# TensorE's attention loop as fourteen bodies written out, in a gated cross-attention and feed-forward kernel

## The reference, cut to what matters

```python
x = x + tanh(g_xattn) * mha(layernorm(x), ctx, ctx)      # x, ctx: 32 x 256 x 512, 16 heads of 32
x = x + tanh(g_ffn) * ffn(layernorm(x))                  # ffn: 512 -> 1408 (silu(gate) * up) -> 512
# mha: q, k, v projections with bias, softmax(q k^T / sqrt(32)) v, output projection with bias
# ffn: weights and activations are rounded to 8-bit grids; the scale of the activations
# is the maximum over the whole tensor, so each of its two quantisations needs a pass of its own
```

## Time and profile before

| | us |
|---|---|
| three runs | 1904.65, 1897.21, 1901.03 |
| their median | 1901.03 |
| the profiled execution's own time | 1898.31 |
| its span, first to last instruction | 1896.1 |
| PE's granted clock, mean of the span | 0.951 of full speed |
| T of body 1, start of body 2 | 191.4 |
| T of body 15, start of body 16 | 1269.4 |

### The profile page before, as it was taken

The page is one execution under the profiler, slowest core; times in us unless marked ns, Lnnn a source line. Parts: engine busy times, 40 slices in busy tenths (PEclk is TensorE's granted clock), DMA queues, the critical chain, the costliest instruction groups (busy, mean ns, idle before and its releaser), DMA issues.

```text
span 1896.1 us, 34665 instructions
## 1 busy us (share of the span) xinstructions
PE 1645.5 (87%) x11820; PEld 782.3 (41%) x11868; DVE 1402.2 (74%) x1853; ACT 813.1 (43%) x1068; POOL 516.7 (27%) x782
## 2 busy tenths in 40 slices
PE   3769989989999899998999899986599999989787
PEld 2224434434344344443444434433344444434333
DVE  6627687787877868768778687786778778878565
ACT  2223524325144152342432514324677777756242
POOL 6212414324133242331422423112000000006644
PEclk7979999999999999999999999998799999999899
DMA  6445454454444444445445444315235453115997
GB/s 190 127 119 116 121 147 110 121 138 120 126 109 121 135 119 125 115 119 148 110 121 127 128 126 93 94 55 204 89 142 192 166 214 140 45 45 212 340 420 301
DMA packets 271525, 274.48 MB, mean 145 GB/s; under 512 B 156720, under 2 KB 205872, under 8 KB 268848
## 3 DMA queue, kind: packets, MB, share of 16 engines
q1 hardware_dynamic: 271408, 272.73, 47.4%
HBM read 126.10 MB, written 62.39 MB: 99 GB/s over the span
## 4 chain that ended last, share of the span: by engine, by line
issue 63%; POOL 13%; DVE 9%; PE 6%; DMA 4%; SPq 2%; POOLq 1%; ACT 0%; DVEq 0%; ACTq 0%
DMA x<-out_dram 4%; DVE rs L873 3%; POOL ol L545 3%; POOL xres L552 3%; POOL yh L600 3%; PE bank L1264 2%; DVE mx L881 2%; SPq L358 1%; PE bank L1165 1%; POOL nw L527 1%; PE bank L1167 1%; PE bank L1166 1%; POOLq L259 1%; POOL nw L525 1%; POOL nw L529 1%
## 5 line engine op out<-in xcount | busy, mean ns | idle before, releaser
L873 DVE RECIPROCAL rs<-bank 128x256 f32<-128x256 f32 x128 | 224.5, 1754 | 125.7 <-POOL ol L545 105.5
L639 ACT ACTIVATE pr<-spair 128x1024 f32<-128x1024 f32 x256 | 258.9, 1019 | 112.0 <-PE spair L1246 112.0
L881 DVE TENSOR_REDUCE mx<-spair 128x4 f32<-128x1024 f32 x256 | 300.0, 1213 | 0.0
L632 ACT ACTIVATE parts<-bank,bqk 128x512 f16<-128x512 f32 x128 | 87.9, 687 | 293.9 <-PE bank L1167 293.9
L1264 PE MATMUL bank<-pr,v 128*32 128x256 f32 x2048 | 140.5, 392 | 54.8 <-DVE o L875 54.8
L1361 PE MATMUL spair<-xqT,wgT 128*128 128x512 bf16 x684 | 179.5, 382 | 2.8 <-ACT xqT L747 1.8
L1361 PE MATMUL spair<-xqT,wuT 128*128 128x512 bf16 x691 | 179.9, 381 | 0.7
L860 DVE SCALAR_TENSOR_TENSOR parts<-bank,bqk,parts 128x512 f16<-128x512 f32 x128 | 95.1, 748 | 114.6 <-ACT parts L632 114.6
L1246 PE MATMUL spair<-stacks 128*128 128x256 f16 x1024 | 154.1, 277 | 7.8 <-DMA stacks<-mT 7.3
L1165 PE MATMUL bank<-xT,wqT 128*128 128x512 f16 x256 | 103.2, 403 | 58.8 <-issue 24.7
L730 ACT ACTIVATE sil<-spair,gsc 128x512 f32<-128x512 f32 x176 | 118.1, 680 | 75.2 <-PE spair L1361 75.2
(11 more groups left out here) (160 smaller groups left out, 3198.6 us busy)
## 6 DMA issues: line engine op xcount, KB each, us to landing
stacks<-parts SPq DMA_DIRECT2D x768, 64.0 KB, 2.0
x<-out_dram SPq DMA_DIRECT2D x32, 1024.0 KB, 11.2
h_spill<-hb SPq DMA_DIRECT2D x10, 2816.0 KB, 9.2
hb<-h_spill SPq DMA_DIRECT2D x10, 2816.0 KB, 15.2
xbuf<-in_x_dram SPq DMA_DIRECT2D x16, 1024.0 KB, 5.4
cbuf<-in_ctx_dram SPq DMA_DIRECT2D x16, 1024.0 KB, 6.0
xres<-in_x_dram SPq DMA_DIRECT2D x16, 1024.0 KB, 5.3
out_dram<-xres SPq DMA_DIRECT2D x16, 1024.0 KB, 4.3
```

What stands on the lines that cost most here:

```text
L639: act.activation(pr[:, u % 4, :, :, :].rearrange("p a b q -> p (a b q)"), spair[u % 2][:, :, :].rearrange("p a q -> p (a q)"), ACT.Exp, sc ...
L873: dve.reciprocal(rs[:, g % 2, :], obank[:, S:2 * S]).then_inc(recip_done, 1)
L881: dve.tensor_reduce(mx[:, h:h + 2, b, :], spair[u % 2][:, :, :].rearrange("p a (q k) -> p a q k", q=KH), AX_X, ALU.max).then_inc(max_done, 1)
```

## The change

PE's loop over i from 1 to 7, with two bodies in each iteration, becomes fourteen bodies in a row. The loop is a Python `for` now, which writes its instructions out when the program is built. PE's branch and its loop register are gone, the values in the waits are constants, and so the `waits_passed` increments behind the waits marked `alone` aren't issued by PE in these bodies. The matmuls, their order and what each waits for are the same. The programs of the other engines are the same.

```diff
             body(1, 0, 1, None)
-            with pe.Fori(1, NG // 2) as i:
-                body(2 * i, 2 * i - 1, 0, 2 * i - 2)
-                body(2 * i + 1, 2 * i, 1, 2 * i - 1)
+            for i in range(2, NG):
+                body(i, i - 1, i % 2, i - 2)
             body(None, NG - 1, None, None)
```

## The result

| | before | after |
|---|---|---|
| median of 20 runs, us | 1902.67 | 1891.76 |
| lowest to highest | 1892.04 to 1911.60 | 1888.75 to 1897.21 |
| ratio after to before, 95% interval | | 0.9948 (0.9933 to 0.9962) |
| span of the profiled execution | 1896.1 | 1890.6 |

The kernel got faster, by 0.52% in the ratio and by 10.9 us in the medians, where 17.0 were forecast and 8.0 to 26.0 lay inside the range. The twenty runs of after also lie in less than half the width of the twenty before.

What follows compares the result with a forecast made beforehand. PE, the fullest engine, was taken as the bound. Bodies 4 to 14 go from 853.0 to 829.4 plus 6.6 for the clock, 836.0: 17.0 us saved, profiled 1881.3, plus 2.7 for the median, 1884.0; range 1875 to 1893.

Steps and rivals of the forecast that it cites:

- The six turns: Seams ahead of bodies 4, 6 to 14: each loop turn costs 3.3 us net at the second `pv`; all six go.
- Rival B: At the seams: the stall is not the turn's; only 1.4 us go, time 1900 us; chance 0.06.
- D: Rival in bodies 2 to 15: fetching straight code starves PE; 1944 us at 1 us per late packet; chance 0.03.
- The clock's term: Last third of bodies 4 to 14: lower granted clock costs 1.2 us in 5.5 of eleven bodies, 6.6 us.
- The ends: Limits of the lower-clock cost in bodies 4 to 14: none of them pays, or all eleven do.
- only two lengths: Odd bodies take either 75.4 us at clock 1.00 or 76.6 us at 0.98, nothing else.
- Constants instead of registers: Waits in the fourteen bodies: constants change nothing; at the end 0.15 us a body either way, 2 us.
- Rival C: Bodies 4 to 15 all pay 1.2 us of clock, constants cost 2 us: 7.2 us gained, 1894 us; chance 0.09.
- A: The forecast case: six turns go, the clock's cost falls on some bodies; 1877 to 1891 us; chance 0.81.

Runs made afterwards that it cites:

- the tiny loops at the seams: Written-out kernel with a two-pass loop of one semaphore increment at each of the six seams where the loop used to turn: 1892.15 us, ratio to before 0.9951.
- the kernel that turns once: Bodies 2 and 3 written out, 4 to 15 as a six-body loop run twice with register waits, against the kernel before: 1887.09 us, ratio 0.9929.
- the shifted loop: Kernel before with 128 semaphore increments on PE ahead of the loop and body 1, so the loop lies later in the program: 1902.44 us, ratio 1.0028.
- the two written-out kernels: Written-out kernel with ten unread matmuls a body in PE's pauses, 1879.02 us; the same with max_pair's two waits swapped as well, 1874.59 us.
- the looped one: Kernel before, with its loop and register waits, plus the ten unread matmuls in each body's pauses: 1902.09 us, ratio 0.9999.

## Why the prediction was right, and where it was off

**The six turns** went as the prediction had it: 18.7 us are gone from bodies 4 to 14, the second `pv` stops the gain at 15.3 us after T (15.1 forecast, from a T that came 0.24 us later), the first twelve matmuls take 2.6 us at 1.00, and PE's waits on L875 rose by 5.7 us (8 forecast). Its 3.3 us a turn was read off body 4 alone and does not hold for the two turns at 2.4 to 2.5; the sum escaped this because it went by the whole 853.0 us. That it is the far target and not the branch was shown by the tiny loops at the seams; that fetching is what takes the time is argued. The rows agree with it: 5, 4 and 5 packets of instructions in bodies 2, 3 and 4, where it had been 7 around body 4, and 85 instead of 97 in all, the 6 x 2 fewer that the prediction named. In the kernel that turns once it is 7 packets in body 10 and 4 or 5 in each other body. Against a simple price by the packet: part of the twelve goes with the shorter program (34027 counted instructions instead of 34665), and the shifted loop has 6 packets in each body behind a turn and 5 in the others, with the same gaps. Rival B, a stall that is not the turn's, is out, and so is D: there is no issue gap in the straight code.

**The clock's term** was mis-sized: 6.6 us were taken, 10.9 measured in the profiled execution and 8.3 in the second. Seven of the eleven bodies pay in either, where 5.5 were taken, and on average 1.6 and 1.2 us. The ends, 0 and 13.2, held. The step that failed is that there are "only two lengths": a third, 78.2, pays 2.4 to 2.5 us. The step before it, that the profile of before shows the usual share of long bodies, was the weaker one. That profile is one of the faster executions, 1898.3 against a median of 1902.67, and the shifted loop shows that a kernel with the same loop can also run with bodies of about 79.2 and 77.8 in turn. That the clock's term hangs on PE's idle time ahead of the last `pv` was shown by filling the two pauses: in the two written-out kernels all of bodies 2 to 14 are free of it, and in the looped one five of six odd bodies.

**Constants instead of registers** were taken at nothing, with 0.15 us a body as the end. They cost 0.28 a body, 3.9 us over fourteen. The comparison of body 1 with body 3 ran from the fourth to the eighth `pv`, where both took 22.34 us. It held only one of the `max_pair`s that lose 0.09, and this one stands ahead of a wait for DVE that swallows it: the rows showed it as 1.64 against 1.74 us at the eighth `pv`, and I read the difference as no cost. The cost lies behind it, in the stretch that I compared for its clock alone. Constants also brought T forward by 0.24 us in each body, which nothing was waiting for.

**What it comes to.** The measured 1891.76 lies 7.8 us above the 1884.0 that was forecast. The constants are 3.9 of it, the clock's larger share 1.7 by one profile and 4.3 by the other, which makes 5.6 to 8.2. Of the gain only 17.0 - 10.9 = 6.1 us are missing, because the 1901.03 of three runs became 1902.67 of twenty, 1.6 us in the change's favour by luck. Rival C, given 0.09, had named just these two terms and 1894 us; the truth lies between A and C, and nearer to C. It lies 0.8 us outside A's own 1877 to 1891, and inside the whole range for the 2 us that had been added at its end for the constants.

## What to carry to other kernels

A loop's turn can be priced in one trace by comparing the bodies behind it with their neighbours; take what the next engine gives back off it, and unroll where the seam is exposed. Straightening one engine's program doesn't give the neighbours' stretch back: where TensorE idles for a microsecond or two in each body behind another engine, look at the granted clock, and try matmuls that nobody needs. Here they helped only in the straight program. Compare undisturbed bodies to 0.01 us and not only their sum: 0.28 us a body is invisible in a span that scatters by ten, and is 4 us at the end.

## What the runs showed of the hardware that was not expected

- Ten added matmuls a body, in pauses of 1.2 and 1.7 us, kept the granted clock at 1.00 in bodies 2 to 14 and made these bodies and body 15 together 8.4 to 11.0 us shorter.
- Of two waits on constants ahead of one matmul, the order is worth 0.09 us where one of them is late.
- A semaphore increment by itself cost PE 0.15 us where it had no cover.
- A taken branch to near code was free in a pause of 1.6 us, while a turn over two bodies left a gap of 3.6 to 3.9 us, which in one kernel grew to 6.1 for a reason that stays open.
- Turns with nearly equal gaps had two prices. In the kernel before four cost 3.2 to 3.6 us and two 2.4 to 2.5, with gaps of 3.6 to 3.9 us in both groups; the clock behind the gap goes with it (0.53 over 4.8 us in body 4, 0.73 over 5.2 us in body 6). What decides between them stays open: in the kernel before and in the shifted loop the cheap ones stand behind long bodies, but the one turn of the six-body loop, behind a body of 76.4, cost 3.6.
